# A state-space block on one core: X turned by DMA, step sizes moved into the exponents, one bank ring laid out anew

## The reference

```python
# B = 8 sequences of 1024 tokens, 256 features; 8 heads of 64, state 64; INNER = 512
x = x + layernorm(attn(layernorm(x)))
x = x + layernorm(ffn(layernorm(x)))

def attn(u):
    x = u @ Wx.T; z = u @ Wz.T                       # 256 -> 512 each
    x = silu(causal_conv(x, conv_w, conv_b))         # 4 taps
    b = (x @ Wb.T).reshape(bsz, seq, HEADS, STATE)   # 512 -> 512
    c = (x @ Wc.T).reshape(bsz, seq, HEADS, STATE)
    dt = softplus(x @ Wdt.T + b_dt)                  # one step size per head
    a = -exp(log_a)
    # scan over the tokens, per head:
    state = exp(dt_t * a) * state + (dt_t * b_t)[:, None] * x_t[None, :]
    y_t = c_t @ state
    y = y + d_param * xh
    yn = (y - mean) / sqrt(var + EPS) * gn_w + gn_b  # over all tokens of a head
    return (yn * silu(z)) @ Wout.T

def ffn(u):     # weights are mean(|w|) * sign(w), row by row
    return gelu(u @ w1b.T + b1) @ w2b.T + b2         # 256 -> 1024 -> 256
```

## Time and profile before

| | before |
|---|---|
| median of 3 runs | 1265.96 us (1265.4 to 1268.12) |
| profiled execution, device time | 1265.6 us |
| its span | 1263.9 us |
| granted TensorE clock, mean | 0.997 of full speed |
| TensorE busy | 1218.3 us (96%) |
| VectorE busy | 997.3 us (79%) |
| ScalarE busy | 878.6 us (70%) |
| GpSimd busy | 465.5 us (37%) |
| DMA queue q1, share of 16 engines | 14.9% |

### The profile page before, as it was taken

One profiled execution on the slowest core, in us unless ns is written; L12 is line 12 of the kernel. 1 busy time (PEld: TensorE's weight loads), 2 busy tenths in 40 slices (PEclk: granted clock), 3 DMA queues, 4 the chain that ended last, 5 costly groups with the idle time before them and its releaser, 6 DMA issues.

```text
span 1263.9 us, 27616 instructions
## 1 busy us (share of the span) xinstructions
PE 1218.3 (96%) x10306; PEld 765.1 (61%) x10306; DVE 997.3 (79%) x2385; ACT 878.6 (70%) x1554; POOL 465.5 (37%) x557
## 2 busy tenths in 40 slices
PE   7999999999999999999999999999999999999896
PEld 5665657565565756656566565756656575564674
DVE  6666877788787796978779787778878789787687
ACT  6675677667776687766966678667787668776365
POOL 2131236142451524416343243623336152441332
PEclk9999999999999999999999999999999999999999
DMA  8011101111020110202111020111112111020001
GB/s 239 1 35 36 34 17 35 43 42 36 18 68 17 35 34 18 68 18 53 26 41 35 18 68 18 35 38 26 55 17 52 34 18 34 18 68 17 2 1 51
DMA packets 91829, 48.09 MB, mean 38 GB/s; under 512 B 63120, under 2 KB 89892, under 8 KB 91696
## 3 DMA queue, kind: packets, MB, share of 16 engines
q1 hardware_dynamic: 91696, 46.33, 14.9%
HBM read 22.72 MB, written 8.39 MB: 25 GB/s over the span
## 4 chain that ended last, share of the span: by engine, by line
PE 76%; DVE 14%; issue 5%; ACT 2%; POOL 2%; DVEq 0%; ACTq 0%; POOLq 0%
PE bank L1728 34%; PE bank L1945 8%; PE bank L1928 8%; PE bank L1837 5%; PE bank L1815 4%; PE bank L1899 3%; DVE xs L1303 3%; PE bank L1905 3%; PE bank L1873 3%; PE bank L1807 2%; PE bank L1860 2%; PE bank L1851 2%; DVE gn_stats L1442 2%; DVE yT L1481 1%; PE bank L1826 1%
## 5 line engine op out<-in xcount | busy, mean ns | idle before, releaser
L937 POOL TENSOR_TENSOR Cd<-Cd,CT 128x512 f32<-128x512 f32 x64 | 93.8, 1465 | 359.8 <-ACT Cd L1180 359.4
L1728 PE MATMUL bank<-sh,WbT 128*128 128x512 f16 x768 | 171.5, 379 | 1.9 <-DVE sh L1308 1.2
L1728 PE MATMUL bank<-sh,WcT 128*128 128x512 f16 x768 | 171.3, 379 | 0.0
L1208 ACT ACTIVATE hf<-bank,vectors,alpha 128x512 f32<-128x512 f32 x128 | 99.0, 776 | 52.0 <-PE bank L1928 30.2
L1303 DVE SCALAR_TENSOR_TENSOR xs<-xi,vectors,xs 128x512 f32<-128x512 f32 x168 | 125.1, 749 | 9.4 <-ACT xs L1085 5.7
L1728 PEld LDWEIGHTS bank<-sh,WcT 128*128 128x128 f16 x768 | 75.2, 98 | 86.6
L1728 PEld LDWEIGHTS bank<-sh,WbT 128*128 128x128 f16 x768 | 72.9, 98 | 87.1 <-DVE sh L1308 6.1
L1928 PE MATMUL bank<-uh,sign1T 128*128 128x512 f16 x512 | 121.6, 380 | 1.8 <-issue 1.7
L1945 PE MATMUL bank<-sign2T,hh 128*128 128x256 f16 x1024 | 117.2, 273 | 1.2 <-DVE hh L1543 1.1
L1945 PEld LDWEIGHTS bank<-sign2T,hh 128*128 128x128 f16 x1024 | 97.8, 98 | 21.7 <-ACT hf L1208 6.5
L868 POOL TENSOR_TENSOR rstd_mid<-var_eps_mid,power 128x4 f32<-128x4 f32 x16 | 16.2, 1011 | 227.3 <-DVE var_eps_mid L1258 227.3
(11 more groups left out here) (235 smaller groups left out, 2600.1 us busy)
## 6 DMA issues: line engine op xcount, KB each, us to landing
xt<-L_attn_input_tensor_dram SPq DMA_DIRECT2D x17, 512.0 KB, 4.1
u<-L_attn_input_tensor_dram SPq DMA_DIRECT2D x15, 512.0 KB, 3.9
out_dram<-u SPq DMA_DIRECT2D x15, 512.0 KB, 3.0
yT<-in_L_ffn_w_dram SPq DMA_DIRECT2D x2, 512.0 KB, 8.8
u<-in_L_ffn_w_dram SPq DMA_DIRECT2D x2, 512.0 KB, 9.3
BT<-in_L_attn_Wx_dram SPq DMA_DIRECT2D x1, 512.0 KB, 5.1
BT<-in_L_attn_Wz_dram SPq DMA_DIRECT2D x1, 512.0 KB, 4.5
zs<-in_L_attn_Wb_dram SPq DMA_DIRECT2D x1, 512.0 KB, 6.2
```

Source lines behind the costliest of these rows:

```text
L937: pool.tensor_tensor(Cd[n % 2][:, :, :], Cd[n % 2][:, :, :], CT[:, :, q * P:(q + 1) * P], ALU.mult)\
L1208: nc.scalar.activation(hf[f % 2][:, :], bank(t, ("H", j, f))[:, :], ACT.Gelu, bias=b1_col[:, f:f + 1], scale=alpha1[:, f:f + 1]).then_inc( ...
L1728: mm = nc.tensor.matmul(bank(t, key)[:, :], w[i][:, k, cols(m)], v[h][:, k, :], start=(a == 0), stop=(a == len(terms) - 1))
```

## The change

It does five things. (1) The four TensorE transposes of `xs` in each chunk and their bank are gone. In their place SP issues two DMA transposes for each chunk, one of each f16 half of `xs`, into `x_turned`, which lies in two unused rows of `xi`; the halves `sh` are stored chunk by chunk for it. Chunks 0 and 1 are turned after the halves are made, chunks 2 and 3 once VectorE has read chunks 0 and 1. (2) `xdt` is now the sum of the two turned halves, without the step size. (3) The step size goes into the exponents as a logarithm: a new Ln on ScalarE ("ln_dt"), a floor and two widening instructions on VectorE ("ln_wide"), and a second f32 matmul into the banks of "cums" and of "sums". (4) The own ring has two empty places before block 0 and three before block 1, where there was one before each; with X gone from it the keys fall on other banks. (5) "end_tiles" stands behind "carry" and "back" of chunk 1 and no longer ahead of them. In block 0 the Gelu table is loaded after the folds, in both blocks after the new Ln. Some small buffers share their place.

```diff
-        steps += own(("log", j))
-        steps += tail(("mid_norm", j)) + own(("B", j, 1), ("decay", j)) + tail(("gelu_table",))
+        steps += own(("X", j, 0), ("X", j, 1), ("log", j))
+        steps += tail(("mid_norm", j)) + own(("B", j, 1), ("decay", j)) + tail(*[("fold", 1, m) for m in range(2 if j == 0 else 0)])
         steps += (own(("head_stat", 0, 1)) + weights(("alpha1", 0), ("ready", 0))) if first and j else []
-        steps += tail(*[("fold", 1, m) for m in range(2 if j == 0 else 0)], ("ff_stat", j))
+        steps += own(("ln_dt", j)) + tail(("gelu_table",), ("ff_stat", j)) + own(("ln_wide", j))
...
-        steps += own(("score", j, 1), ("carry", j, 0)) + norm + (own(("head_stat", 0, 0)) if j else [])
+        steps += own(("X", j, 2), ("score", j, 1), ("X", j, 3), ("carry", j, 0)) + norm + (own(("head_stat", 0, 0)) if j else [])
...
-        steps += own(("E", j, 2), ("ends", j, 2), ("seg", j, 2), ("front", j, 2), ("score", j, 2)) + end(("end_tiles", j))
-        steps += own(("carry", j, 1), ("back", j, 1), ("E", j, 3), ("ends", j, 3), ("seg", j, 3), ("front", j, 3))
+        steps += own(("E", j, 2), ("ends", j, 2), ("seg", j, 2), ("front", j, 2), ("score", j, 2), ("carry", j, 1), ("back", j, 1))
+        steps += end(("end_tiles", j)) + own(("E", j, 3), ("ends", j, 3), ("seg", j, 3), ("front", j, 3))
...
+        x_turned = [xi[:, KI - 1 if r else 0, 0:BLK].bitcast(F16).rearrange("p (i c f) -> p i c f", i=2, c=KI) for r in range(2)]
...
-        sh = [sb(f"sh{i}", [P, KI, BLK], F16) for i in range(2)]
+        sh_rows = [sb(f"sh{i}", [P, NQ, KI, P], F16) for i in range(2)]
+        sh = [v[:, :, :, :].rearrange("p q c t -> p c q t") for v in sh_rows]
...
+        dt_floor, log_dt = dt_raw, log_u
+        log_wide = sb("log_wide", [P, HP, PARTS, NQ * KI])
...
-                return [*[("seg", *at, g) for g in range(HP)], ("X", *at), ("Bt", *at)]
+                return [*[("seg", *at, g) for g in range(HP)], ("Bt", *at)]
...
-                own_keys.append(None)
+                own_keys.extend([None] * (2 + at[0]))
...
+            def turn_tokens(t, j, q):
+                n = ch(j, q)
+                r = q % 2
+                s, sj, sq = two_before(t, n)
+                if q == 0:
+                    sp.wait_ge(*conv_out.count(t, (j + 1) * KI * (TAPS - 1)))
+                    sp.wait_ge(*sh_hi.count(t, (j + 1) * KI))
+                    sp.wait_ge(*sh_lo.count(t, (j + 1) * KI))
+                sp.wait_ge(*xdt_out.count(s, ch(sj, sq) + 1))
+                for i in range(2):
+                    sp.dma_start_transpose(x_turned[r][:, i, :, :], sh_rows[i][:, q, :, :].rearrange("p c t -> p (c t)")).then_inc(x_rows[r].sem, 16)
...
+                    act.wait_ge(*xdt_out.count(s, (sj + 1) * NQ))
...
+            def step_size_log(t, j):
+                act.wait_ge(*ln_in.count(t, j + 1))
+                nc.scalar.activation(log_dt[:, :, :], dt_floor[:, :, :], ACT.Ln, scale=1.0 / SX).then_inc(ln_out.sem, 1)
...
+                nc.vector.tensor_scalar(dt_floor[:, :, :], dt_t[:, :, :], DT_FLOOR, None, ALU.max).then_inc(ln_in.sem, 1)
...
+            def step_wide(t, j):
+
+                p, pj = before_block(t, j)
+                dve.wait_ge(*full(p, ("cums", pj)))
+                dve.wait_ge(*ln_out.count(t, j + 1))
+                raw = log_dt[:, :, :].rearrange("p q h -> p (q h)")
+                for g in range(HP):
+                    v = of_side(raw, g)[:, None].to_broadcast([P, PARTS // 2, NQ * KI // 2, 2])
+                    nc.vector.tensor_scalar(log_wide[:, g, PARTS // 2:PARTS, :].rearrange("p m (n f) -> p m n f", f=2), v, -1.0, None,
+                                            ALU.mult).then_inc(ln_wide.sem, 1)
...
-                for need in latest(full(t, ("X", j, q)), full(s, ("Y", sj, sq, HP - 1))):
-                    dve.wait_ge(*need)
+                dve.wait_ge(*full(s, ("Y", sj, sq, HP - 1)))
                 dve.wait_ge(*xdw_out.count(s, ch(sj, sq) + 1))
-                nc.vector.tensor_tensor(xdt[r][:, :, :], heads(bank(t, ("X", j, q))[:, :]), per_head(dt_t[:, q, :]),
-                                        ALU.mult).then_inc(xdt_out.sem, 1)
+                dve.wait_ge(*x_rows[q % 2].count(t, n // 2 + 1))
+                hi, lo = [x_turned[q % 2][:, i, :, :].rearrange("p c f -> p (c f)") for i in range(2)]
+                nc.vector.tensor_tensor(xdt[r][:, :, :], heads(hi), heads(lo), ALU.add).then_inc(xdt_out.sem, 1)
...
-                    mm = nc.tensor.matmul(bank(t, key)[:, :], w[i][:, k, cols(m)], v[h][:, k, :], start=(a == 0),
+                    mm = nc.tensor.matmul(by_chunk(bank(t, key)[:, :]), w[i][:, k, cols(m)], v[h][:, k], start=(a == 0),
...
-                                 start=True, stop=True).then_inc(full_sem(t, key), 1)
+                                 start=True, stop=False)
+                pe.wait_ge(*ln_wide.count(t, (j + 1) * HP))
+                nc.tensor.matmul(bank(t, key)[:, 0:P], log_wide[:, :, :, :].rearrange("p g a n -> p (g a n)"), ident[:, :],
+                                 start=False, stop=True).then_inc(full_sem(t, key), 1)
...
-                nc.tensor.matmul(bank(t, key)[:, 0:NQ * HEADS], after[:, :], da[:, :], start=True, stop=True)
+                nc.tensor.matmul(bank(t, key)[:, 0:NQ * HEADS], after[:, :], da[:, :], start=True, stop=False)
+                pe.wait_ge(*ln_out.count(t, j + 1))
+                nc.tensor.matmul(bank(t, key)[:, 0:NQ * HEADS], ident[:, :], log_dt[:, :, :].rearrange("p q h -> p (q h)"),
+                                 start=False, stop=True)
...
-                for name, src in (("X", xs), ("Bt", BT)):
-                    key = (name, j, q)
-                    for need in latest(empty(t, key), B_out.count(t, (j + 1) * KI), C_out.count(t, (j + 1) * KI)):
-                        pe.wait_ge(*need)
-                    for c in range(KI):
-                        mm = nc.tensor.transpose(bank(t, key)[:, cols(c)], src[:, c, cols(q)], ident[:, :])
-                    mm.then_inc(full_sem(t, key), 1)
+                key = ("Bt", j, q)
+                for need in latest(empty(t, key), B_out.count(t, (j + 1) * KI), C_out.count(t, (j + 1) * KI)):
+                    pe.wait_ge(*need)
+                for c in range(KI):
+                    mm = nc.tensor.transpose(bank(t, key)[:, cols(c)], BT[:, c, cols(q)], ident[:, :])
```

More of the change, by code:

```diff
@@ L36 @@
 DECAY_FLOOR = -110.0
+DT_FLOOR = 2.0 ** -52
 PAST = -30000.0
@@ L738, in _ @@
                     signal.prime(sp)
-            for signal in (xh_hi, xh_lo, uh_hi, uh_lo):
+            for signal in (xh_hi, xh_lo, uh_hi, uh_lo, *x_rows):
                 signal.prime(sp)
```

50 lines of the change are left out of this document (34 added, 16 removed).

## The result

| | before | after |
|---|---|---|
| median | 1265.99 us (1265.15 to 1268.18) | 1268.36 us (1266.61 to 1270.99) |
| ratio to before | | 1.0016, 95% interval 1.0009 to 1.0022 |
| span of the profiled execution | 1263.9 us | 1265.0 us |
| TensorE busy | 1218.3 us | 1197.9 us |
| VectorE busy | 997.3 us | 1016.4 us |

The changed kernel is slower by 2.4 us, 0.16%: inside the 0.2% that I had called no change, and 15 us above the forecast. The 20 runs of the changed kernel fall in two groups, 5 at 1266.6 to 1267.0 us with a granted clock of 0.997 to 0.998 (the profiled one is among them) and 15 from 1268.1 us on with 0.993 to 0.994, so part of the 2.4 us goes with the clock; the spans of the two profiled executions differ by 1.1 us.

A forecast was written before the change was run, and what follows sets the result against it. TensorE bounds in the mean, with a second chain (VectorE, GpSimd, ScalarE, DMA) ending level. -28.2 + 5.8 - 4.8 + 8 + 7 = -12.2 us gave a forecast of 1253.5 us, range 1238 to 1269 for 8 in 10.

The forecast's parts named there:

- What speaks against the change: Chunks 2 and 3: `xdt` and GpSimd's `Cd`, both reading SBUF, block each other; 0.5 us a block, 8 us lost.
- the second rival: Slower by the port: `xdt` waits for `Cd` in chunks 2 and 3, 1.82 us a block; 1274.9 us, 16%.
- What TensorE gives back: Split of the next input, behind GpSimd's root and ScalarE's normalising: 0.44 us a block lost again, 7.0 us.
- the first rival: TensorE is the bound throughout and VectorE follows by using its waits; -27.2 us, 1238.8 us, 24%.
- The transposes: TensorE, all 64 chunks: four transposes of `xs` take 0.44 us a chunk; 28.2 us less.
- The second products: TensorE, between the f16 halves and H: new products for "cums" and "sums", 0.36 us a block, 5.8 us more.
- The end statistics: Moved behind chunk 1's additions, they free the bank of TensorE's exponents earlier; 0.3 us a block, 4.8 us gained.
- The moving operand: TensorE's 2,304 products for B, C, xi and z, now read in four pieces of 128: cost 0.
- The DMAs: 128 transposes of X issued by SP, with 6 us to spare before chunk 3's `xdt`: cost 0.
- the fourth rival: The turned X comes late, for example with transposes landing one by one; 1269.4 us at 1 us a block, 2%.
- The third rival: VectorE's chain gets no shorter and the saving turns into waits of TensorE; about 1264 us, 10%.
- the main step: Step to be wrong if blocks get shorter by 1.6 us or more each, or not at all.

The follow-up runs named there:

- e1: Changed kernel, but `xdt` adds one turned half of X in SBUF to a bank, low half of X left out; 1255.94 us, ratio 0.9922.
- e2: Changed kernel with the sum `xdt` moved from VectorE to GpSimd, nothing left out; 1265.61 us, ratio 0.9994.
- e4: Kernel before without TensorE's transposes of `xs` (X left out, `xdt` from the bank of the turned B), with the changed kernel's ring; 1246.78 us, ratio 0.9845.
- e8: Changed kernel without Ln, floor, widening and second products (step size left out of the result); 1262.59 us, ratio 0.9968.
- e14: e1 without Ln, floor, widening and second products (step size and low half of X left out); 1250.76 us, ratio 0.9883.
- e10: Changed kernel with the end statistics in their old place, ahead of the additions of chunk 1; 1269.41 us, ratio 1.0027.
- e3: Changed kernel without the 128 DMA transposes of X, `xdt` adding the unturned halves; 1268.92 us, ratio 1.0024.

## Why the prediction was wrong

**The step that failed** is the term "What speaks against the change": 0.5 us a block, 8 us, between bounds of 0 and 1.8. It measures 19.0 us (1.2 a block) with the statistics in the old place and 11.9 in the new one, both as lower bounds. The mechanism was the one named, its size and its place were off. The choice within the bounds rested on who waits: I let GpSimd be the one, since it "has slack". In chunk 2 it went as the second rival had it: `Cd` goes first, 1.09 us more for `xdt`. In chunk 3 the rival's 0.54 us did not come: `Cd` was done at 514.30 us, `xdt` began at 515.06. What I did not see is chunk 1, where `xdt` stands beside `y` and `Cd`; I had looked only at the chunks with the unbroken VectorE. I had the earlier trace rows with the 2.16 us of `Cd` (it ended 1.14 us after the split, not 1.3 as I wrote). GpSimd has slack in the mean, but `xdw`, the scaled state and the next input's root stand in line behind `Cd` on it, and each is waited for.

On who wins, the traces show the order of the starts: the split started at 508.04 us, `Cd` at 508.51, `xdt` at 509.19, and they were served so; in chunk 1 it was `y` (498.59), `xdt` (499.20), `Cd` (499.83). In chunk 2 the `Cd` that came during the split goes ahead of VectorE's next instruction, in 14 of 16 blocks, and that is the case in which VectorE pays. The Trainium skill (SBUF — State Buffer, "Who interferes with whom") has the one that issues first take the shared ports for its whole instruction while the other waits. By that rule too `xdt` waits in chunk 2 and `Cd` in chunk 1; the trace agrees.

**What TensorE gives back**: 7.0 us forecast, by the way of root, normalising and what follows. The waits for the `Cd` exponential that stay without a stretched `xdt` are 7.2 us in e1 and e2, 7.9 in e4, without the 3.0 us near the end. Right in mechanism and in size. In time e4 gives back 28.2 less 19.6, 8.6 us, but its own wait (6.0 us) can be part of that. These waits also show the first rival (TensorE the bound throughout) wrong.

**The transposes**: TensorE's busy time in e4 is 1190.5 us, 27.8 less; 28.2 was right. **The second products**: 5.8 us forecast; 6.1 in e8, 4.9 in e14. Right. **The end statistics**: -4.8 forecast; -3.8 in the kernel before, so the reading of the chain was fair, but only -1.4 in the changed kernel, where the state is late by the port. I had added the terms as if they were independent; by the times alone the difference of 2.4 us is hardly beyond the uncertainty, but the waits for the state in e10 show the move behind a late `xdt`. **The moving operand**: the mean of its products is 379 ns in both, 768 each for B and C: 0. **The DMAs**: 0, by e3. Nothing waits for them, and the fourth rival did not come. **xdt** free of GpSimd: 0.68 us against 0.69.

**The third rival** (the savings turn into waits, about 1264 us) is the nearest in time and right that the blocks do not get shorter, but the port that the second names is the larger part of the reason. Of the signs that I had set, TensorE's busy time fell by 20.4 us, `xdt` has a mean over 0.9 us, the new waits are for the state and for what is behind the norm, and the blocks did not get shorter, the sign that the main step is wrong. H begins 3.56 us behind its last transpose's issue (558.50 and 554.94) without a wait, so that chain has gained 0.4 us of slack instead of setting the end.

The forecast summed to -12.2 us; with the measured port (+19.0 for 8), 8.6 for 7.0 and -1.4 for -4.8 the sum is +3.8, beside a result of +2.0 to +2.4. This is no independent check: it is the chain of the table with my 5.8 us in place of its +4.0. The wait that the substitutes bring lies in the 8.6 and is missing from the 19.0, so it falls out of the sum.

What stays open: why the early mean costs the kernel before 2.7 us, and how much more than 19 us (11.9 in the new place) the port is worth, since the substitute has a wait of its own.
